# Decoder layer on one core: VectorE's share of the softmax exponentials, from 15 units of degree five in twelve passes to 19 units in eight instructions

## The chip, the cores and the metric

The kernel runs on one core of a Trainium2 chip. The metric is device time in microseconds (us) of one execution, as the median of several runs.

## What is computed

One decoder layer in float32: a small self-attention over distances, a cross-attention of 1024 query rows to 6404 context rows with 16 heads of width 8, and a quantized feed-forward part, each followed by a layer norm. Nearly all the time goes to the cross-attention:

```python
qh = split_heads(q @ Wq + bq)
kh = split_heads(k @ Wk + bk)
vh = split_heads(v @ Wv + bv)
logits = einsum('bhsd,bhtd->bhst', qh, kh) / sqrt(8)
attn = softmax(logits, axis=-1)
out = einsum('bhst,bhtd->bhsd', attn, vh)
```

These are 16 x 1024 x 6404, some 105 million exponentials.

## The kernel before

**Work.** A phase is one group of four heads and one half (512) of the query rows: eight phases. The 6404 context rows are 51 tiles of 128, in 17 chunks of three tiles (NC = 17). A tile and a head make one unit of 128 x 512 logits, one PSUM bank. Three units make a block: four blocks per chunk (BPC), three in the last chunk, 67 per phase, 536 in all. A block uses banks 0 to 2 or 3 to 5 by turns; banks 6 and 7 hold the accumulators. The logits are made with the context rows on the partitions, so the exponentials go straight into the values matmul; the row sums come from a column of ones beside the values.

**Engines.** TensorE goes through the blocks in order (`chunk`, L1320): it waits for the probabilities of two blocks before (probs_ready, L1340), writes a block's scores S (`scores`, twelve matmuls, L1284) and then does a part of the values V of the chunk before (`values`, L1314: eight matmuls of 512 for a tile, seen as 16 in the profile; the middle tile is done in two halves of 256 columns). ScalarE takes the exponential of each block in one instruction (`exponentials`, L706 to L712) of 1536 columns, or of 1024 where VectorE does the last unit. VectorE does that unit in the block s = 2 of 15 chunks of a phase (chunk 0 and chunks 2 to 15): `take` (L952) rounds the logit to an integer (e_t) and subtracts it (e_f), both out of PSUM; `power` (L970) evaluates a polynomial in the rest by Horner's rule (e_u) and multiplies it with the power of two (e_pow), which GpSimd makes from e_t (`powers`, L585). Every pass is cut into two halves of 256 columns, so that one half works while the result of the other becomes visible: twelve instructions. GpSimd also copies a chunk's values into v_op (`stage`, L577). The sync engine loads the keys (`load_k`, L279).

**Order and waits.** Before the first block of a chunk TensorE waits until VectorE has read the scores of the unit two blocks before (L1338, e_step), and before the values of the third tile until that unit's probabilities are written (L1365, e_probs). Chunks 2 to 13 run in a hardware loop of four chunks (KS) on TensorE, and of two on ScalarE; there the waits compare with registers. VectorE and GpSimd are written out. Between phases VectorE reads the accumulators (`add_acc`, L943; it needs the last values of the phase), and TensorE waits for that before the first values of the new phase (L1361).

```python
for s in range(LAST_BPC if c == NC - 1 else BPC):
    if s == 0 and c:
        wait(e_step, at(E_STEPS * (e_count(ph, c - 1) - 1) + E_TAKEN, E_STEPS))
    wait(probs_ready, at(f + s + 1, BPC))
    scores(m % KS, q, ph, c == NC - 1, s)
```

## Time and profile before

| | |
|---|---|
| median of 3 runs | 834.43 us (834.39 to 834.64) |
| profiled execution | 833.03 us |
| its span, first to last instruction | 831.3 us |
| mean granted TensorE clock | 0.967 |
| ScalarE busy | 736.0 us (89%) |
| TensorE busy | 707.7 us (85%) |
| VectorE busy | 689.5 us (83%) |
| GpSimd busy | 174.9 us (21%) |

The profile names the engines PE (TensorE matmuls), PEld (its weight loads), DVE (VectorE), ACT (ScalarE), POOL (GpSimd) and SP (sync). "L710" is line 710 of the kernel. A length in a timeline runs from the start of the first instruction of a row to the end of the last, xN is their count, and the brackets at its end tell how long the engine stood idle before it, and what ended that. Lengths of neighbours overlap: on ScalarE and VectorE the next instruction starts before the last one's results are all written.

### The profile page before, as it was taken

Reading aid. Unit: us, or ns where it says so; the run is one execution under the profiler, and the core shown is the slowest. Engines: PE = TensorE matmul, PEld = TensorE weight load, DVE = VectorE, ACT = ScalarE, POOL = GpSimd, SP = SyncE. Lnnn points to the kernel's source line nnn. Section 1 sums busy time; section 2 is a strip of 40 time slices with the busy share of each in tenths; the row PEclk is TensorE's granted clock in tenths of the full one; section 3 lists DMA queues with packets and bytes.
Section 4 is the critical chain, followed back from the end, with each engine's and each line's share of the span. In section 5 each row is a group of like instructions: output and inputs, shape, how many; then the busy total and the mean of one; then the engine's idle time right before and its main releaser. Section 6 shows DMA issues by size and latency. Waiting matters only on the chain.

```text
span 831.3 us, 38425 instructions
## 1 busy us (share of the span) xinstructions
PE 707.7 (85%) x15210; PEld 319.9 (38%) x15212; DVE 689.5 (83%) x1952; ACT 736.0 (89%) x650; POOL 174.9 (21%) x304
## 2 busy tenths in 40 slices
PE   6996679899899998899998999888899998899841
PEld 3445434443444344334443444344433443344321
DVE  3518767996999699969996999699978997899766
ACT  2436879999999999999999999999999999999741
POOL 2501511221222122212221222122212221222100
PEclk9998989999999999999999999999999999999965
DMA  3303521111111111111111111111111111111000
GB/s 105 83 25 107 170 86 37 37 43 44 38 36 45 42 37 38 43 43 38 36 44 43 36 37 40 44 38 35 40 48 35 37 37 49 37 36 38 14 1 26
DMA packets 36611, 38.41 MB, mean 46 GB/s; under 512 B 8430, under 2 KB 35088, under 8 KB 36512
## 3 DMA queue, kind: packets, MB, share of 16 engines
q1 hardware_dynamic: 35644, 36.59, 14.8%
q8 instruction: 65, 1.06, 0.5%
q10 hardware_dynamic: 868, 0.48, 0.2%
q14 instruction: 34, 0.28, 0.1%
HBM read 30.15 MB, written 6.42 MB: 44 GB/s over the span
## 4 chain that ended last, share of the span: by engine, by line
ACT 40%; issue 24%; PE 16%; SPq 10%; DVE 5%; DMA 3%; POOL 1%; ACTq 1%; POOLq 0%; DVEq 0%
ACT probs L710 39%; SPq L291 8%; PE ps L1314 6%; PE ps L1284 3%; PE ps L1213 2%; PE ps L1199 2%; DMA k_op<-k_parts_dram 2%; SPq L505 1%; DMA k_parts_dram<-k_parts 1%; PE ps L1162 1%; DVE stats L776 1%; PE ps L1449 1%; ACTq L723 1%; POOL k_parts L541 0%; DMA q_parts_dram<-q_parts 0%
## 5 line engine op out<-in xcount | busy, mean ns | idle before, releaser
L710 ACT ACTIVATE probs<-ps 128x1536 f32<-128x1536 f32 (+1 forms) x536 | 671.7, 1379 | 11.9 <-PE ps L1284 11.4
L1314 PE MATMUL ps<-probs,v_op 64*9 64x512 f32 (+1 forms) x8384 | 523.5, 494 | 13.8 <-DMA k_op<-k_parts_dram 9.1
L1284 PE MATMUL ps<-q_op,k_op 59*32 59x512 bf16 x6432 | 337.4, 382 | 60.7 <-ACT probs L710 56.4
L979 DVE SCALAR_TENSOR_TENSOR e_u<-e_u,e_f 128x256 f32<-128x256 f32 x720 | 259.2, 425 | 0.0
L1284 PEld LDWEIGHTS ps<-q_op,k_op 59*32 59x32 bf16 x6432 | 107.9, 90 | 331.5 <-issue 245.7
L1314 PEld LDWEIGHTS ps<-probs,v_op 64*9 64x9 f32 x8384 | 169.3, 86 | 90.2 <-issue 27.7
L588 POOL TENSOR_SCALAR e_pow<-e_t 128x512 int32<-128x512 int16 x120 | 74.4, 620 | 353.9 <-DVE e_t L960 353.9
L960 DVE TENSOR_SCALAR e_t<-ps 128x256 f32<-128x256 f32 x240 | 90.5, 418 | 60.5 <-PE ps L1284 51.3
L581 POOL COPY v_op<-v_all 128x108 f32<-128x108 f32 x136 | 68.3, 502 | 181.3 <-PE ps L1314 180.6
L979 DVE SCALAR_TENSOR_TENSOR e_u<-e_f 128x256 f32<-128x256 f32 x240 | 90.1, 416 | 0.2
L986 DVE SCALAR_TENSOR_TENSOR probs<-e_u,e_pow 128x256 f32<-128x256 f32 x240 | 89.6, 411 | 0.0
L966 DVE SCALAR_TENSOR_TENSOR e_f<-ps,e_t 128x256 f32<-128x256 f32 x240 | 89.2, 413 | 0.0
L541 POOL TENSOR_TENSOR k_parts<-probs,k_parts 128x384 bf16<-128x384 f32 x17 | 17.6, 1038 | 66.2 <-ACT k_parts L640 66.2
L667 ACT ACTIVATE probs<-ps,neg_n 128x1024 f32<-128x1024 f32 x8 | 8.9, 1113 | 16.8 <-PE ps L1213 16.8
L1162 PE MATMUL ps<-ctx_t,wk_turned 128*128 128x384 f32 x34 | 16.6, 571 | 6.3 <-ACT ctx_t L619 3.3
L1009 DVE STREAM_TRANSPOSE att_rows<-acc_t 128x512 f32<-128x512 f32 x7 | 5.0, 711 | 15.6 <-DMA o_t<-att_rows 15.6
L627 ACT ACTIVATE kf<-ps,bias_cols 128x384 f32<-128x384 f32 x17 | 9.8, 578 | 8.9 <-PE ps L1162 8.9
L1165 PEld LDWEIGHTS ps<-wv_sb,ctx_t 128*128 128x128 f32 x102 | 15.5, 208 | 5.2 <-issue 1.2
L1213 PE MATMUL ps<-y_rhs,y_lhs 64*128 64x512 f32 x32 | 15.6, 611 | 0.7 <-DVE v_all L811 0.7
L811 DVE TENSOR_TENSOR v_all<-ps,bv_bc 128x384 f32<-128x384 f32 (+1 forms) x17 | 9.4, 555 | 7.8 <-PE ps L1165 7.8
L640 ACT ACTIVATE k_parts<-probs 128x384 bf16<-128x384 f32 x17 | 8.8, 519 | 8.0 <-DVE probs L826 8.0
L1199 PE MATMUL ps<-probs,x_nat 128*128 128x512 f32 x32 | 15.6, 615 | 0.0
(177 smaller groups left out, 257.7 us busy)
## 6 DMA issues: line engine op xcount, KB each, us to landing
k_op<-k_parts_dram SPq DMA_DIRECT2D x544, 36.0 KB
k_parts_dram<-k_parts SPq DMA_DIRECT2D x17, 288.0 KB, 2.5
k_op<-k_parts_dram SPq DMA_DIRECT2D x272, 12.0 KB
ctx_nat<-in_ctx_dram SPq DMA_DIRECT2D x16, 192.0 KB, 2.6
q_op<-q_parts_dram SPq DMA_DIRECT2D x32, 48.0 KB
q_parts_dram<-q_parts SPq DMA_DIRECT2D x2, 384.0 KB, 3.4
x_nat<-in_x_dram SPq DMA_DIRECT2D x1, 512.0 KB, 3.9
o_t<-att_rows SPq DMA_DIRECT2D x28, 16.0 KB
```

Of the source, the lines that this page charges most:

```text
L291: sp.dma_start(k_op[W2 * r + a:W2 * r + a + DH * copies, slot, :, :].rearrange("p i t -> p (i t)"), bass.AP(src.tensor, starts[part][r], [ ...
L581: pool.tensor_copy(v_op[:, slot].rearrange("p j (h d) -> p j h d", h=G), v_all[:, bass.ds(tile, CT), head:head + G, :]).then_inc(v_staged, 1)
L588: pool.tensor_scalar(e_pow[:], e_low(e_t[:]), float(2 ** 23), float(EXP2_LEAD), ALU.mult, ALU.add).then_inc(e_pow_ready, 1)
L710: act.activation(probs[:, b % NP].rearrange("p u t -> p (u t)")[:, 0:columns], ps[:, bank:bank + BU, :].rearrange("p u t -> p (u t)")[:, 0 ...
L960: dve.tensor_scalar(e_t[:, cols], score, E_MIN, ROUND, ALU.max, ALU.add).then_inc(e_step, 1)
L966: dve.scalar_tensor_tensor(out=e_f[:, cols], in0=score, scalar=E_MIN, in1=e_low(e_t[:, cols]), op0=ALU.max, op1=ALU.subtract).then_inc(e_s ...
L979: dve.scalar_tensor_tensor(out=e_u[:, cols], in0=u[:, cols], scalar=a, in1=e_f[:, cols], op0=ALU.add, op1=ALU.mult).then_inc(e_step, 1)
L986: dve.scalar_tensor_tensor(out=probs[:, block % NP, BU - 1, 512 - EW + cols.start:512 - EW + cols.stop], in0=e_u[:, cols], scalar=EXP2[0], ...
L1199: last = pe.matmul(ps[:, 4 + b, :], x_nat[:, j, :], attn_e[:, j, HQ * b:HQ * b + HQ], start=(j == 0), stop=(j == TQ - 1), skip_group_check ...
L1213: last = pe.matmul(ps[:, 2 * (j % 2) + b, :], y_lhs[:, P * j:P * j + P], y_rhs[:, HQ * b:HQ * b + HQ], start=True, stop=True)
L1284: return pe.matmul(ps[a:a + P // G, bank, :], k_op[W2 * r:W2 * r + KR, kslot, i, P * j + a:P * j + a + P // G], q_op[W2 * r:W2 * r + KR, q ...
L1314: last = pe.matmul(ps[32 * k:32 * k + DH + 1, ACC[h], a:b], v_op[W2 * h:W2 * h + W2, slot, j, (DH + 1) * k:(DH + 1) * (k + 1)], probs[W2 * ...
```

## The change

VectorE makes 19 units per phase instead of 15, at places listed in E_AT (chunk, block): (0, 0), then in each turn of four chunks the blocks (0, 2), (1, 1), (2, 0), (2, 3), (3, 2), and at the end (14, 2), (15, 1), (16, 0). In these blocks ScalarE has 1024 columns. The polynomial is evaluated in another form: u = (f + a) f in two halves, f' = (u + c) f in two halves, f' scaled as (f' + d) times the power of two in one pass of 512 (`scale`), and the product (u + b) times that in one pass of 512 (`finish`). Rounding and remainder (e_t, e_f) are one pass of 512 each, so a unit has eight instructions. The scale of a unit is issued behind e_t of the next one, and the finish behind its e_f; e_f, e_u and e_pow have two buffers, in memory shared with qf and qr. ScalarE's loop has four chunks. TensorE waits for e_taken two blocks behind each unit, and makes the values of a tile between six and eight blocks after the tile's scores. After the last block the values of two more tiles are left, and the last ones wait for the last unit.

```diff
--- before.py
+++ after.py
@@ -74,16 +74,21 @@
 QSCALE = SCALE * LOG2E
 EW = 512
 EH = EW // 2
-E_BLOCK = BPC - 2
-E_UNITS = NC - 2
-EXP2_LEAD = 0x3aae0400
-EXP2 = [753.2197875976562, 522.0919799804688, 180.93934631347656,
-        41.8090705871582, 7.287810325622559]
+E_LOOP = 4
+E_TURN = ((0, 2), (1, 1), (2, 0), (2, 3), (3, 2))
+E_FIRST = 2
+E_AT = ([(0, 0)] + [(c + k, t) for c in range(E_FIRST, NC - 3, E_LOOP) for k, t in E_TURN] +
+        [(NC - 3, 2), (NC - 2, 1), (NC - 1, 0)])
+E_UNITS = len(E_AT)
+EXP2_OFF = 2
+EXP2_LEAD = 0x3a8bec00 - EXP2_OFF * 2 ** 23
+EXP2 = [9.525652885437012, 28.199888229370117, 45.54460906982422, 132.23011779785156]
 E_MIN = -116.0
-E_STEPS = 12
-E_TAKEN = 4
+E_STEPS = 5
+E_AHEAD = 1
...
+        q_work = sb("q_work", [P, 4, HQ])
...
+        qf, qr = q_work[:, 0:2, :], q_work[:, 2:4, :]
+        e_f = [e_f0[:], q_work[:, 0, :]]
+        e_u = [e_u0[:], q_work[:, 1, :]]
+        e_pow = [e_pow0[:], q_work[:, 2, :].bitcast(I32)]
...
+            def powers(ph, c, t):
+
+                n = e_count(ph, c, t)
+                pow2 = e_pow[n % 2]
+                if n > 2:
+
+                    pool.wait_ge(e_probs, E_AHEAD + n - 2)
+                pool.wait_ge(e_rounded, n)
+                pool.tensor_scalar(pow2, e_low(e_t[:]), float(2 ** 23), float(EXP2_LEAD),
                                    ALU.mult, ALU.add).then_inc(e_pow_ready, 1)
 
             for ph in range(PHASES):
                 for c in range(NC):
                     m = ph * NC + c
-                    stage(m % 2, m, c * CT, ph % NG * G)
-                    if c != 1 and c < NC - 1:
-                        powers(ph, c)
+                    for t in range(BPC):
+                        if t == 2:
+                            stage(m % 2, m, c * CT, ph % NG * G)
+                        if (c, t) in E_AT:
...
+                f = ph * BPP + c * BPC
+                for t in range(LAST_BPC if c == NC - 1 else BPC):
+                    count = f + t + 1 + AHEAD
+                    exponentials(f + t, count if i is None else i * (E_LOOP * BPC) + count,
+                                 BU * 512 - EW if (c, t) in E_AT else BU * 512)
 
             for ph in range(PHASES):
-                f = ph * BPP
-                for s in range(BPC):
...
-                    exponentials(f + s, f + (s + 1 + AHEAD))
-                with act.Fori(0, E_UNITS // 2) as r:
-                    for s in range(2 * BPC, 4 * BPC):
-                        exponentials(f + s, r * (2 * BPC) + (f + s + 1 + AHEAD), shared(s % BPC))
-                for s in range((NC - 1) * BPC, BPP):
-                    exponentials(f + s, f + (s + 1 + AHEAD))
+                for c in range(E_FIRST):
+                    chunk(ph, c)
+                with act.Fori(0, (NC - 3 - E_FIRST) // E_LOOP) as i:
+                    for c in range(E_FIRST, E_FIRST + E_LOOP):
+                        chunk(ph, c, i)
...
+            def make_probs(ph, at, before):
+
+                def score(block):
+                    return ps[:, BU * (block % 2) + BU - 1, :]
+
+                n = e_count(ph, *at)
+                block = ph * BPP + at[0] * BPC + at[1]
+                f, u = e_f[n % 2], e_u[n % 2]
+                if n > 1:
+
+                    dve.wait_ge(e_pow_ready, n - 1)
                 dve.wait_ge(scores_done, block + 1 + AHEAD)
+                dve.tensor_scalar(e_t[:], score(block), E_MIN, ROUND + EXP2_OFF, ALU.max, ALU.add
+                                  ).then_inc(e_rounded, 1)
+                if before:
+                    scale(*before)
+                dve.wait_ge(e_rounded, n)
+                dve.scalar_tensor_tensor(out=f, in0=score(block), scalar=E_MIN, in1=e_low(e_t[:]),
+                                         op0=ALU.max, op1=ALU.subtract).then_inc(e_taken, 1)
+                if before:
+                    finish(*before)
+                for i, cols in enumerate(halves):
+                    dve.wait_ge(e_taken, n)
+                    dve.scalar_tensor_tensor(out=u[:, cols], in0=f[:, cols], scalar=EXP2[0],
+                                             in1=f[:, cols], op0=ALU.add, op1=ALU.mult
...
+                for i, cols in enumerate(halves):
+                    dve.wait_ge(e_step, E_STEPS * (n - 1) + i + 1)
+                    dve.scalar_tensor_tensor(out=f[:, cols], in0=u[:, cols], scalar=EXP2[2],
+                                             in1=f[:, cols], op0=ALU.add, op1=ALU.mult
+                                             ).then_inc(e_step, 1)
+
+            def scale(ph, at):
+
+                n = e_count(ph, *at)
+                f = e_f[n % 2]
+                dve.wait_ge(e_pow_ready, n)
+                dve.wait_ge(e_step, E_STEPS * (n - 1) + 4)
+                dve.scalar_tensor_tensor(out=f, in0=f, scalar=EXP2[3], in1=e_pow[n % 2].bitcast(F32),
+                                         op0=ALU.add, op1=ALU.mult).then_inc(e_step, 1)
+
+            def finish(ph, at):
+
+                n = e_count(ph, *at)
+                block = ph * BPP + at[0] * BPC + at[1]
+                dve.wait_ge(e_step, E_STEPS * n)
+                dve.scalar_tensor_tensor(out=probs[:, block % NP, BU - 1, :], in0=e_u[n % 2],
+                                         scalar=EXP2[1], in1=e_f[n % 2], op0=ALU.add, op1=ALU.mult
+                                         ).then_inc(e_probs, 1)
...
+                for n, at in enumerate(E_AT):
+                    make_probs(ph, at, (ph, E_AT[n - 1]) if n > 1 else
+                               (ph - 1, E_AT[-1]) if ph and n == 0 else None)
+                    if n == 0:
+                        scale(ph, at)
+                        finish(ph, at)
+                        if ph:
+                            add_acc(ph - 1)
+                            turn_acc()
+                            if ph > 1:
+
+                                dve.wait_ge(o_written, 16 * G * (ph - 1))
+                            dve.transpose(att_rows[:], acc_t[:].rearrange("p n d -> p (n d)")
+                                          ).then_inc(att_ready, 1)
+            scale(PHASES - 1, E_AT[-1])
+            finish(PHASES - 1, E_AT[-1])
...
-            def chunk(ph, c, i=None, reach=0):
+            def chunk(ph, c, i=None):
...
                 def at(count, step):
-                    return count if i is None else pe.to_reg(i * (reach * step) + count)
+                    return count if i is None else pe.to_reg(i * step + count)
...
+                def wait_unit(signal, ahead, ph_u, c_u, t):
+
+                    turn = 0 if i is None else 1
+                    if (c_u + turn * E_LOOP, t) in E_AT:
+                        n = e_count(ph_u, c_u + turn * E_LOOP, t) - turn * len(E_TURN)
+                        wait(signal, at(ahead + n, len(E_TURN)))
+
+                def made(back, j, a=0, b=HQ, count=1, first=False):
+
+                    ph_v, c_v = (ph, c - back) if c >= back else (ph - 1, c - back + NC)
+                    if ph_v < 0:
+                        return
+                    if j == 0:
+
+                        wait(v_staged, at(m - back + 1, KS))
+                    if a == 0:
+                        for t in range(BPC):
+                            if (t * BU + BU - 1) // G == j:
+                                wait_unit(e_probs, E_AHEAD, ph_v, c_v, t)
+                    values((m - back) % 2, ph_v * BPP + c_v * BPC, j, c_v == NC - 1, count, first, a, b)
+
                 for s in range(LAST_BPC if c == NC - 1 else BPC):
-                    if s == 0 and c:
-
-                        wait(e_step, at(E_STEPS * (e_count(ph, c - 1) - 1) + E_TAKEN,
-                                        E_STEPS))
-                    wait(probs_ready, at(f + s + 1, BPC))
+                    if c or s >= 2:
+                        wait_unit(e_taken, 0, ph, *((c, s - 2) if s >= 2 else (c - 1, s + 2)))
+                    elif ph:
+                        wait_unit(e_taken, 0, ph - 1, NC - 1, s + 1)
+                    wait(probs_ready, at(f + s + 1, KS * BPC))
                     scores(m % KS, q, ph, c == NC - 1, s)
...
-                        wait(v_staged, at(m, 1))
+                        wait(k_loaded[(m + 1) % KS], at(K_LOAD * ((m + 1) // KS + 1), K_LOAD))
                     if c == 0:
-                        if s < CT:
-                            values(slot, f - LAST_BPC, s, True, count=2 if s == 1 else 1)
-                    elif c == NC - 1:
-                        if s == 2:
-                            pe.wait_ge(e_probs, 2 * e_count(ph, c - 1))
-                        values(slot, f - BPC, s, False, count=2 if s == 1 else 1)
+                        if s < 2:
+                            made(2, s + 1, count=2 - s)
+                        else:
+                            made(1, s - 2, count=s - 1)
+                    elif c == 1 and s < 2:
+                        if s == 0:
+                            made(2, 2)
                     elif s == 0:
+                        made(2, 1, a=HQ // 2)
+                    elif s == 1:
+                        made(2, 2)
+                    elif s == 2:
                         if c == 1 and ph:
 
                             pe.wait_ge(acc_step, ACC_STEPS * (ph - 1) + 2)
-                        values(slot, f - BPC, 0, False, first=c == 1)
-                    elif s == 3:
-
-                        wait(e_probs, at(2 * e_count(ph, c - 1), 2))
-                        values(slot, f - BPC, 2, False)
+                        made(1, 0, first=c == 1)
                     else:
-                        values(slot, f - BPC, 1, False, a=(s - 1) * (HQ // 2), b=s * (HQ // 2))
+                        made(1, 1, b=HQ // 2)
...
+            last_m = PHASES * NC - 1
+            pe.wait_ge(e_probs, E_AHEAD + E_UNITS * PHASES - 1)
+            for j in range(1, CT):
+                values((last_m - 1) % 2, BLOCKS - LAST_BPC - BPC, j, False, count=3 - j)
             pe.wait_ge(o_written, 16 * G * NG)
             pe.wait_ge(probs_ready, BLOCKS + 1)
             project_out(0)
             pe.wait_ge(v_staged, PHASES * NC)
+            pe.wait_ge(e_probs, E_AHEAD + E_UNITS * PHASES)
             for j in range(CT):
                 pe.wait_ge(probs_ready, BLOCKS + min(j + 1, 2))
-                values((PHASES * NC - 1) % 2, BLOCKS - LAST_BPC, j, True, count=2 if j == 1 else 1)
+                values(last_m % 2, BLOCKS - LAST_BPC, j, True, count=2 if j == 1 else 1)
```

The old `take` and `power` (L952 to L989) go, and so does the old order of the phase on VectorE (L1000 to L1012).

## Rows read from the trace of the kernel before

**Rows 1.** The page of the profile, part 1: busy time of each engine.
```profile
PE 707.7 (85%) x15210; PEld 319.9 (38%) x15212; DVE 689.5 (83%) x1952; ACT 736.0 (89%) x650; POOL 174.9 (21%) x304
```

**Rows 2.** Windows, phase 2: length, then busy PE, PEld, DVE, ACT, POOL; clock.
```profile
275.25:359.26 84.01, 76.00 (x1862) 32.76 (x1852) 75.81 (x216) 83.81 (x69) 17.25 (x32) 1.00 0.14 40
```

**Rows 3.** Windows, the steady loop of phase 3 (twelve chunks), columns as before.
```profile
372.26:431.53 59.27, 53.66 (x1356) 24.68 (x1344) 58.10 (x168) 59.27 (x49) 13.65 (x24) 1.00 0.13 38
```

**Rows 4.** Timeline of ACT, one chunk: start us, length us, instruction.
```profile
381.22 1.47 ACT L710 ACTIVATE probs<-ps 128x1536 f32<-128x1536 f32 x1
382.55 1.05 ACT L710 ACTIVATE probs<-ps 128x1024 f32<-128x1024 f32 x1
383.50 1.45 ACT L710 ACTIVATE probs<-ps 128x1536 f32<-128x1536 f32 x1
384.84 1.45 ACT L710 ACTIVATE probs<-ps 128x1536 f32<-128x1536 f32 x1
386.17 1.47 ACT L710 ACTIVATE probs<-ps 128x1536 f32<-128x1536 f32 x1
387.50 1.05 ACT L710 ACTIVATE probs<-ps 128x1024 f32<-128x1024 f32 x1
```

**Rows 5.** Timeline of PE, the same chunk: L1284 scores, L1314 values.
```profile
381.49 0.61 PE L1284 MATMUL ps<-q_op,k_op 59*32 59x512 bf16 x12 [0.18 <-ACT probs L710]
...
382.84 0.61 PE L1284 MATMUL ps<-q_op,k_op 59*32 59x512 bf16 x12 [0.30 <-ACT probs L710]
...
384.04 0.61 PE L1284 MATMUL ps<-q_op,k_op 59*32 59x512 bf16 x12
384.35 1.16 PE L1314 MATMUL ps<-probs,v_op 64*9 64x512 f32 x16
385.21 0.62 PE L1284 MATMUL ps<-q_op,k_op 59*32 59x512 bf16 x12
385.56 0.70 PE L1314 MATMUL ps<-probs,v_op 64*9 64x256 f32 x16
```

**Rows 6.** Timeline of DVE, the same chunk.
```profile
382.15 0.76 DVE L960 TENSOR_SCALAR e_t<-ps 128x256 f32<-128x256 f32 x2
382.82 0.74 DVE L966 SCALAR_TENSOR_TENSOR e_f<-ps,e_t 128x256 f32<-128x256 f32 x2
```

**Rows 7.** Groups by line and shape, whole execution: busy us, mean ns; idle before.
```profile
L710 ACT ACTIVATE probs<-ps 128x1536 f32<-128x1536 f32 x416 | 575.4, 1471 | 11.9 <-PE ps L1284 11.4
...
L979 DVE SCALAR_TENSOR_TENSOR e_u<-e_u,e_f 128x256 f32<-128x256 f32 x720 | 259.2, 425 | 0.0
...
L588 POOL TENSOR_SCALAR e_pow<-e_t 128x512 int32<-128x512 int16 x120 | 74.4, 620 | 353.9 <-DVE e_t L960 353.9
L960 DVE TENSOR_SCALAR e_t<-ps 128x256 f32<-128x256 f32 x240 | 90.5, 418 | 60.5 <-PE ps L1284 51.3
```

**Rows 8.** Line L979 in the steady loop: shortest, median and longest duration in ns.
```profile
L979 DVE SCALAR_TENSOR_TENSOR e_u<-e_u,e_f x72: 409/414/495, 374.3 to 430.4; 128x256 f32<-128x256 f32 x72
```

**Rows 9.** Timeline of DVE at the start of phase 4: two dependent passes of 512.
```profile
446.79 0.68 DVE L946 COPY acc_sb<-ps 128x512 f32<-128x512 f32 x1
447.50 0.69 DVE L947 TENSOR_TENSOR acc_sb<-acc_sb,ps 128x512 f32<-128x512 f32 x1
```

**Rows 10.** Timeline of all engines where TensorE was held by e_f.
```profile
397.66 0.74 DVE L966 SCALAR_TENSOR_TENSOR e_f<-ps,e_t 128x256 f32<-128x256 f32 x2
...
398.79 0.64 PE L1284 MATMUL ps<-q_op,k_op 59*32 59x512 bf16 x12
...
400.04 0.62 PE L1284 MATMUL ps<-q_op,k_op 59*32 59x512 bf16 x12
```

**Rows 11.** List of waits, whole execution: us in total, times, longest us.
```profile
PEld ps L1284 <- DVE e_f L966: 15.7, 32, 1.0
```

**Rows 12.** Timeline of ACT and of PE at the end of the last phase.
```profile
778.55 5.57 ACT L710 ACTIVATE probs<-ps 128x1536 f32<-128x1536 f32 x4
...
784.20 2.79 PE L1314 MATMUL ps<-probs,v_op 64*9 64x512 f32 x40
```

More of the change, by code:

```diff
@@ L170, in decoder_layer @@
         e_t = sb("e_t", [P, EW])
-        e_f = sb("e_f", [P, EW])
-        e_u = sb("e_u", [P, EW])
-        e_pow = sb("e_pow", [P, EW], I32)
+        e_f0 = sb("e_f", [P, EW])
+        e_u0 = sb("e_u", [P, EW])
+        e_pow0 = sb("e_pow", [P, EW], I32)
         acc_sb = sb("acc_sb", [P, HQ])
@@ L236, in decoder_layer @@
         acc_step, e_step, e_probs = sem("acc_step"), sem("e_step"), sem("e_probs")
+        e_rounded, e_taken = sem("e_rounded"), sem("e_taken")
         e_pow_ready = sem("e_pow_ready")
@@ L266, in row_bc, with e_count @@
             return bass.AP(v.tensor, v.offset, [[0, P], [1, ap.shape[0]]])
-        def e_count(ph, c):
-            return ph * E_UNITS + max(c - 1, 0) + 1
+        def e_count(ph, c, t):
+            return ph * E_UNITS + sum(at <= (c, t) for at in E_AT)
         def e_low(ap):
@@ L869, in _ @@
             chain.step(dve.memset(gmax[:], 0.0))
+            dve.sem_inc(e_probs, E_AHEAD)
             dve.wait_ge(attn_e_ready, TQ)
@@ L1318, in values, with chunk @@
                 last.then_inc(values_done, count)
-            def chunk(ph, c, i=None, reach=0):
+            def chunk(ph, c, i=None):
                 m = ph * NC + c
@@ L1376, in _ @@
                     for c in range(2, 2 + KS):
-                        chunk(ph, c, i, KS)
+                        chunk(ph, c, i)
                 for c in range(NC - 3, NC):
```

60 lines of the change are left out of this document (4 added, 56 removed).

## The prediction

> **What bounds the kernel now.** First the busy table and the windows of the phases. ScalarE leads with 736.0 of 831.3 us [rows 1], and most of the time is eight phases of some 84 us in which it is busy throughout: 83.81 of 84.01 us [rows 2]. In the steady loop (chunks 2 to 13) it never stops, 59.27 of 59.27 us, with VectorE right behind (58.10) and TensorE at 53.66 [rows 3]. A microsecond taken off ScalarE there is a microsecond gained, if neither of the others takes its place. Both are near, so the next thing to read is the handover between the engines, in one chunk of four blocks.
>
> There ScalarE starts the short block b (1024 columns) at 382.55, b+1 at 383.50, b+2 at 384.84, b+3 at 386.17 and the next short one at 387.50 [rows 4]: 0.94 us for a short block, then 1.35, 1.33 and 1.33 for full ones, 4.95 in all. The difference, 0.39, is what one more unit on VectorE saves ScalarE.
>
> Scores S go into two sets of three PSUM banks by turns, so S(b+2) may not start before everybody has read block b. TensorE starts S(b) at 381.49, S(b+1) at 382.84, S(b+2) at 384.04 and S(b+3) at 385.21; the first two had waited for ScalarE [rows 5], which ended block b at 382.55 + 1.05 = 383.60 and b+1 at 384.95 [rows 4]. A block of scores whose banks come free last starts 0.15 after that end: for S(b+1) that end is b-1's, at some 382.69 (381.22 + 1.47). From the start of S to the first instruction that reads it 0.66 us pass: VectorE's e_t of block b starts at 382.15 [rows 6], ScalarE's b+1 at 383.50.
>
> VectorE's unit is now twelve passes of 256. From e_t at 382.15 to the end of e_f at 382.82 + 0.74 = 383.56 it takes 1.41 us; with that the scores are taken. Independent passes of 256 start 0.335 apart (0.67 for two) [rows 6], though each lasts about 0.42 [rows 7]. While GpSimd copies v_op, one pass lasts 0.495 instead of 0.414 [rows 8]: 0.08 more in each chunk.
>
> Call D the start of e_t of unit block b. ScalarE, undisturbed, starts b+2 at 384.84 = D + 2.69. For that S(b+2) must start by D + 2.03. Now it starts at D + 1.89. **The slack is 0.14 us**, and on this point all else turns.
>
> **The change part by part.** (1) ScalarE: four more short blocks per phase, 32 in all, at 0.39 each: 12.5 us less work.
>
> (2) VectorE's unit becomes two passes of 512 on PSUM (e_t, e_f), two of 512 in SBUF (scale, finish) and four of 256. No row has independent 512-wide passes. From below: 256 columns start 0.335 apart, and from 256 to 512 the duration goes from 0.42 to 0.69 [rows 7, 9], 0.27 more, so 0.60. From above: 0.71, the distance of COPY and the TENSOR_TENSOR that needs its result [rows 9]. The change puts another pass between most that depend on each other, which is nearest to the independent rows: 0.60. The unit is 4 x 0.60 + 4 x 0.335 = 3.75, with the copy's share 3.80. Per 16 blocks that is 5 x 3.80 = 19.0, about the 4 x 4.77 of now (12 x 0.335, the gaps to e_t and the copy's share; the page's busy share says the same, 58.10 in twelve chunks).
>
> (3) The order inside a unit is e_t, scale of the unit before, e_f, finish of the unit before. So the scores are taken at D + 0.60 + 0.60 + 0.69 = D + 1.89, not D + 1.41. In its loop TensorE waits first on e_taken, then on probs_ready, both against registers. What such a pair costs when e_f is last stands once in the steady stretch: e_f ends at 397.66 + 0.74 = 398.40 and S starts at 398.79, 0.39 later [rows 10]; 32 waits of this kind are in the list of the whole execution [rows 11]. So S(b+2) starts at D + 2.28 and ScalarE's b+2 at D + 2.94, **0.25 us late**, on an engine without slack. From below: with only the 0.15 that ScalarE's end costs, S(b+2) starts at D + 2.04, on the edge of the slack. The 0.39 is of the same wait, so I take it.
>
> (4) Behind that late S, TensorE is in order: values, then S(b+3), which in four cases of five belongs to the next unit. With a full set of values (16 matmuls of 512) S to S is 1.25 after a late start [rows 10]. With a half set (16 of 256) the next S could start 0.30 before the values end, as it does behind a full one (384.35 + 1.16 against 385.21): 385.56 + 0.70 - 0.30 - 385.21 = 0.75 [rows 5].
>
> (5) One turn of the loop is 16 blocks with units at blocks 2, 5, 8, 11 and 14: distances 3, 3, 3, 3 and 4. ScalarE alone would need 0.94 + 1.35 + 1.33 = 3.62 for a distance of 3. The next e_t comes at the later of VectorE's 3.80 and TensorE's 2.28 + V + 0.66:
> - first and second: a half set follows, 3.69, so VectorE decides: 3.80 each.
> - third and fourth: a full set follows: 4.19 each.
> - the long one: ScalarE starts b+2 at 2.94, ends it 1.45 later [rows 4]; S(b+4) follows at 4.54, e_t at 5.20. VectorE would be free at 3.80 and waits, so what was lost is not won back.
>
> The sum is 21.18 us for 16 blocks, now 4 x 4.95 = 19.79: +1.39, in 24 turns **+33.4 us**.
>
> (6) The other 19 blocks of a phase take 84.0 - 3 x 19.79 = 24.6 now [rows 2]. Then: 3.80 and 3.80, a third distance into the next phase between 3.87 (wait 0.15, full set 1.17) and 4.19, taken as 4.0 because the waits are against constants there, and from unit (0,0) to unit (2,2) ten blocks, one short: 10 x 1.335 - 0.39 = 13.0. Again 24.6: nothing. The accumulators are read two blocks later, and chunk 1 starts on them two blocks later. GpSimd's powers are used a unit after they are made. Both cost nothing under that cover; without it the powers would put their 0.62 plus a handover into each unit.
>
> (7) Tail: the last exp ends at 778.55 + 5.57 = 784.12 and the 40 last value matmuls start at 784.20 [rows 12]. Afterwards the last unit lies on block 533, and without a following unit it ends at D + 3.75 + two dependent passes of 512 (1.45) and a handover, some 5.3, while ScalarE ends at D + 4.2: +1.1.
>
> 833.03 + 33.4 + 1.1 = 867.5 for the profiled execution, which lies 1.4 below the median of the runs: **869 us**.
>
> [...] e_t reads PSUM and lasts 0.418 per 256 columns, e_u works in SBUF alone and lasts 0.425 [rows 7]: PSUM has no price of its own here. [...]
>
> **Rivals.**
> - *Faster: the take is early enough.* If S(b+2) starts by D + 2.03 and a unit takes no more than 3.62, ScalarE stays the bound throughout and only the 12.5 us count: 822. For it: VectorE's work per turn, 19.0, fits under ScalarE's 11 x 1.335 + 5 x 0.94 = 19.39. Against it: the average is not what is asked; three blocks leave 3.62 and a unit takes 3.75 even with no wait. 0.11.
> - *Half of it: TensorE passes it on faster.* With 0.15 for the wait and 1.17 for a full set the distances are 3.80, 3.80, 3.87, 3.87 and 4.96, 20.30 per turn, +12.2, with the tail 848. I count 847 to 855 here: 0.15.
> - *More: the 512-wide passes don't overlap.* At 0.67 apart (two of 256) the unit is 4.10, the take at 2.03: 4.10, 4.10, 4.33, 4.33 and 5.34, 22.2 per turn, +58, 893. Beyond 882: 0.05.
> - *The values wait.* A finish ends 2.5 after the next e_t, 6.7 after its own, and its values are due six blocks, 8 us, after: 1.3 to spare. 0.01.
>
> The forecast, 855 to 882, keeps 0.68. The range takes it and the smaller case in, 847 to 882. Within 0.2% (about what a measurement of this kernel can tell from no change) lies only an accident between the first two cases: 0.02. Faster 0.11, slower 0.87.
>
> **What would show it.** Right: ScalarE's idle time before L710, 11.9 us now [rows 7], rises to some 45, ended by TensorE's scores; TensorE waits on e_f in nearly every unit of the loop, some 120 times; e_t starts 3.8, 3.8, 4.2, 4.2 and 5.2 apart; passes of 512 start 0.60 apart; a phase lasts 88 us. Wrong: ScalarE without idle time in the loop and phases of 82.4 (the first rival), or e_f ending before D + 1.7.

## The result: 855.17 us against 834.53, and the profile after

| | before | after |
|---|---|---|
| median | 834.53 us (834.39 to 834.76, 4 runs) | 855.17 us (854.08 to 856.41, 4 runs) |
| ratio, 95% interval | | 1.0244 (1.0226 to 1.0262) |
| span of the profiled execution | 831.3 us | 853.0 us |
| ScalarE, TensorE, VectorE, GpSimd busy | 736.0, 707.7, 689.5, 174.9 | 738.4, 718.7, 694.5, 275.6 |

The kernel is 2.4% slower; that it would be slower was forecast. The size is 20.6 us where 34.5 were forecast, and 855.2 lies at the very edge of the likeliest case (855 to 882), inside the range of 847 to 882.

ScalarE has 32 short passes more and is still counted busy for 2.4 us longer. The passes themselves became shorter, 1335 ns in the mean of 536 against 1379. But a pass of 1.46 us that is followed at once shares 0.12 us with the next one (they start 1.33 to 1.35 apart in [rows 4]), and one that is followed by a wait is counted in full.

The windows of the kernel after, as in [rows 2] and [rows 3]: phases 0, 2 and 3, and one turn of the loop (16 blocks) in phase 2; length first, then busy PE, PEld, DVE, ACT and POOL.

```profile
101.07:191.21 90.14, 76.38 (x1790) 30.23 (x1784) 73.58 (x152) 84.27 (x67) 31.83 (x37) 0.92 0.17 51
312.78:333.78 21.00, 18.18 (x456) 7.43 (x448) 19.05 (x40) 20.01 (x17) 7.81 (x9) 1.00 0.13 36
...
278.65:365.90 87.25, 77.42 (x1865) 30.79 (x1852) 76.24 (x159) 84.16 (x68) 30.39 (x36) 1.00 0.14 39
365.90:453.91 88.01, 77.87 (x1865) 30.74 (x1852) 76.24 (x159) 84.26 (x68) 30.39 (x36) 1.00 0.14 39
```

In [rows 3] ScalarE had no idle time in the loop; now it stands still for 0.99 of 21.00 us. Each other engine has spare time (VectorE 1.95, TensorE 2.82), and none is the bound by its share. A turn was 4 x 4.947 = 19.79 and is 21.00; a phase was 84.01 and is 87.25.

The timeline of VectorE in that turn, as in [rows 6]: the second unit whole, the starts of the others.

```profile
316.53 0.68 DVE L984 TENSOR_SCALAR e_t<-ps 128x512 f32<-128x512 f32 x1
317.13 0.68 DVE L1010 SCALAR_TENSOR_TENSOR q_work<-q_work 128x512 f32<-128x512 f32 x1
317.73 0.68 DVE L989 SCALAR_TENSOR_TENSOR e_f<-ps,e_t 128x512 f32<-128x512 f32 x1
318.33 0.68 DVE L1018 SCALAR_TENSOR_TENSOR probs<-q_work 128x512 f32<-128x512 f32 x1
318.93 0.75 DVE L995 SCALAR_TENSOR_TENSOR e_u<-e_f 128x256 f32<-128x256 f32 x2
319.60 0.75 DVE L1000 SCALAR_TENSOR_TENSOR e_f<-e_u,e_f 128x256 f32<-128x256 f32 x2
320.27 0.68 DVE L984 TENSOR_SCALAR e_t<-ps 128x512 f32<-128x512 f32 x1
...
321.47 0.68 DVE L989 SCALAR_TENSOR_TENSOR q_work<-ps,e_t 128x512 f32<-128x512 f32 x1
...
324.48 0.69 DVE L984 TENSOR_SCALAR e_t<-ps 128x512 f32<-128x512 f32 x1 [0.31 <-PE ps L1318]
...
328.56 0.69 DVE L984 TENSOR_SCALAR e_t<-ps 128x512 f32<-128x512 f32 x1 [0.25 <-PE ps L1318]
```

Passes of 512 start 0.60 apart and last 0.68. From e_t to the end of e_f it is 318.41 - 316.53 = 1.88 us. The starts of e_t are 3.74, 4.21 and 4.08 apart here, 3.75 ahead of the first and 5.22 behind the last (it ends at 333.78): forecast were 3.80, 3.80, 4.19, 4.19 and 5.20. In the first two distances (3.75 and 3.74) VectorE never waits; ahead of the e_t at 324.48 and the one at 328.56 it waits for TensorE.

TensorE and ScalarE around the same unit, as in [rows 5] and [rows 4]:

```profile
318.75 0.61 PE L1318 MATMUL ps<-q_op,k_op 59*32 59x512 bf16 x12
...
319.53 0.61 PE L1318 MATMUL ps<-q_op,k_op 59*32 59x512 bf16 x12
...
322.50 0.61 PE L1318 MATMUL ps<-q_op,k_op 59*32 59x512 bf16 x12
322.87 1.10 PE L1348 MATMUL ps<-probs,v_op 64*9 64x512 f32 x16
323.73 0.64 PE L1318 MATMUL ps<-q_op,k_op 59*32 59x512 bf16 x12
```

```profile
317.93 1.46 ACT L727 ACTIVATE probs<-ps 128x1536 f32<-128x1536 f32 x1
319.41 1.45 ACT L727 ACTIVATE probs<-ps 128x1536 f32<-128x1536 f32 x1
```

Call the time from the end of the take to the start of the scores that waited for it the handover. The scores two blocks on start at 318.75 and 322.50, 0.34 and 0.35 after the end of e_f (318.41, 322.15). ScalarE starts that block at 319.41 = D + 2.88, 1.48 behind the one before instead of 1.33 to 1.35. Behind the second late start a full set of values follows, and the next scores come 1.23 later.

From the list of waits of the whole execution, against the one row in [rows 11]:

```profile
PE ps L1318 <- DVE q_work L989: 26.7, 37, 2.8
ACT probs L727 <- PE ps L1318: 24.8, 68, 1.7
PE ps L1318 <- DVE e_f L989: 24.0, 36, 1.1
...
PEld ps L1318 <- DVE q_work L989: 20.9, 20, 3.4
PEld ps L1318 <- DVE e_f L989: 18.6, 20, 1.0
...
PE ps L1348 <- DMA k_op<-k_parts_dram: 0.4, 1, 0.4
```

The four rows with L989 (e_f in either buffer) add up to 113 entries, where some 120 waits were forecast, but that is not a count of units: some waits stand there twice, for the matmul and for its weight load (0.30 and 0.80 for the scores at 356.36), and some not at all, because TensorE's values end just as the scores start (at 322.48 for those at 322.50). Counted from the starts, the first 14 of the 15 units of a loop have a handover of 0.34 or 0.35 us almost without exception (102 of 112, and all but one of the others at most 0.40): the take holds TensorE in nearly every unit.

The code outside the loop, where the waits compare with constants, hands over faster. Unit (14, 2) of phase 2, the first one behind the loop, is an example:

```profile
355.62 0.68 DVE L989 SCALAR_TENSOR_TENSOR q_work<-ps,e_t 128x512 f32<-128x512 f32 x1
356.36 0.61 PE L1318 MATMUL ps<-q_op,k_op 59*32 59x512 bf16 x12 [0.30 <-DVE q_work L989]
```

e_f ends at 356.30 and the scores start 0.06 later. All 40 units whose scores two blocks on lie outside the loop (five per phase) have 0.05 or 0.06.

### The profile page after: what moved, and what is told of

It is laid out like the page before. It is cut to its first block, busy times and chain, and to the rows that moved or that the text cites. A ratio compares the mean times of both kernels' runs of the same rounds, so it can differ in the third digit from the quotient of the medians.

```text
span 853.0 us, 38088 instructions
## 1 busy us (share of the span) xinstructions
PE 718.7 (84%) x15212; PEld 302.7 (35%) x15212; DVE 694.5 (81%) x1488; ACT 738.4 (87%) x650; POOL 275.6 (32%) x336
## 4 chain that ended last, share of the span: by engine, by line
PE 49%; DVE 21%; issue 12%; ACT 12%; SPq 2%; POOL 2%; DMA 1%; DVEq 0%; ACTq 0%; POOLq 0%
PE ps L1348 22%; PE ps L1318 19%; ACT probs L727 10%; DVE e_f L1010 4%; DVE q_work L1010 4%; DVE e_f L989 3%; DVE q_work L989 3%; PE ps L1247 2%; PE ps L1233 2%; SPq L301 2%; DVE probs L1018 1%; DVE e_t L984 1%; DVE e_u L995 1%; DVE q_work L995 1%; POOL v_op L591 1%
## 5 line engine op out<-in xcount | busy, mean ns | idle before, releaser
L727 ACT ACTIVATE probs<-ps 128x1536 f32<-128x1536 f32 (+1 forms) x536 | 673.9, 1335 | 29.3 <-PE ps L1318 24.8
L984 DVE TENSOR_SCALAR e_t<-ps 128x512 f32<-128x512 f32 x152 | 104.5, 687 | 87.4 <-PE ps L1318 86.4
L603 POOL TENSOR_SCALAR q_work<-e_t 128x512 int32<-128x512 int16 x76 | 68.2, 897 | 118.6 <-DVE e_t L984 90.2
L995 DVE SCALAR_TENSOR_TENSOR e_u<-e_f 128x256 f32<-128x256 f32 x152 | 58.6, 426 | 0.1
L995 DVE SCALAR_TENSOR_TENSOR q_work<-q_work 128x256 f32<-128x256 f32 x152 | 58.6, 426 | 0.2
L1000 DVE SCALAR_TENSOR_TENSOR q_work<-q_work 128x256 f32<-128x256 f32 x152 | 57.1, 415 | 0.0
L1000 DVE SCALAR_TENSOR_TENSOR e_f<-e_u,e_f 128x256 f32<-128x256 f32 x152 | 57.0, 415 | 0.0
L1010 DVE SCALAR_TENSOR_TENSOR e_f<-e_f,e_pow 128x512 f32<-128x512 f32 x76 | 51.7, 680 | 0.5
L1010 DVE SCALAR_TENSOR_TENSOR q_work<-q_work 128x512 f32<-128x512 f32 x76 | 51.7, 680 | 0.4
L989 DVE SCALAR_TENSOR_TENSOR q_work<-ps,e_t 128x512 f32<-128x512 f32 x76 | 51.9, 682 | 0.2
L989 DVE SCALAR_TENSOR_TENSOR e_f<-ps,e_t 128x512 f32<-128x512 f32 x76 | 51.8, 682 | 0.1
L1018 DVE SCALAR_TENSOR_TENSOR probs<-e_u,e_f 128x512 f32<-128x512 f32 x76 | 51.7, 680 | 0.2
L1018 DVE SCALAR_TENSOR_TENSOR probs<-q_work 128x512 f32<-128x512 f32 x76 | 51.7, 680 | 0.1
```

The source lines that it names most:

```text
L603: pool.tensor_scalar(pow2, e_low(e_t[:]), float(2 ** 23), float(EXP2_LEAD), ALU.mult, ALU.add).then_inc(e_pow_ready, 1)
L727: act.activation(probs[:, b % NP].rearrange("p u t -> p (u t)")[:, 0:columns], ps[:, bank:bank + BU, :].rearrange("p u t -> p (u t)")[:, 0 ...
L984: dve.tensor_scalar(e_t[:], score(block), E_MIN, ROUND + EXP2_OFF, ALU.max, ALU.add).then_inc(e_rounded, 1)
L989: dve.scalar_tensor_tensor(out=f, in0=score(block), scalar=E_MIN, in1=e_low(e_t[:]), op0=ALU.max, op1=ALU.subtract).then_inc(e_taken, 1)
L995: dve.scalar_tensor_tensor(out=u[:, cols], in0=f[:, cols], scalar=EXP2[0], in1=f[:, cols], op0=ALU.add, op1=ALU.mult).then_inc(e_step, 1)
L1000: dve.scalar_tensor_tensor(out=f[:, cols], in0=u[:, cols], scalar=EXP2[2], in1=f[:, cols], op0=ALU.add, op1=ALU.mult).then_inc(e_step, 1)
```

## The experiments

Ten more kernels were run, in three groups; each ratio is to the kernel before on the same chip. Six of the medians (swap to old_take5) rest on two runs each, so small differences are read from the distances. D is the start of a unit's e_t. The distances named are those of successive e_t in an undisturbed turn of the loop, each taken from that run's trace.

| run | median us | before, same chip | ratio | one turn of the loop, us |
|---|---|---|---|---|
| swap | 844.1 | 833.8 | 1.0123 (1.0094 to 1.0153) | 3.75, 3.74, 4.01, 3.88, 5.03 = 20.41 |
| early | 861.5 | 833.8 | 1.0332 (1.0237 to 1.0426) | 3.88, 3.95, 3.94, 3.94, 5.03 = 20.74 |
| four | 851.8 | 833.8 | 1.0216 (1.0175 to 1.0257) | 4 x 5.22 = 20.9 |
| four_early | 847.5 | 833.8 | 1.0164 (1.0134 to 1.0193) | 4 x 5.04 = 20.2 |
| old_take6 | 874.9 | 833.4 | 1.0498 (1.0451 to 1.0544) | 4 x 5.35 = 21.4 |
| old_take5 | 845.3 | 833.4 | 1.0143 (0.998 to 1.0305) | 4 x 5.01 = 20.0 |
| four_early2 | 835.7 | 833.4 | 1.0045 (1.0004 to 1.0086) | 4 x 4.95 = 19.8 |
| wide512 | 836.1 | 833.4 | 1.0024 (1.0008 to 1.0039) | 3.74, 3.81, 3.81, 3.73, 4.97 = 20.06 |
| four_wide_swap | 836.4 | 834.8 | 1.0027 (1.0002 to 1.0051) | 4 x 4.98 = 19.9 |
| old_swap | 835.2 | 834.8 | 1.0001 (0.9979 to 1.0024) | 4 x 4.95 = 19.8 |

### The handover: swap

```diff
 for s in range(LAST_BPC if c == NC - 1 else BPC):
+    wait(probs_ready, at(f + s + 1, KS * BPC))
     if c or s >= 2:
         wait_unit(e_taken, 0, ph, *((c, s - 2) if s >= 2 else (c - 1, s + 2)))
     elif ph:
         wait_unit(e_taken, 0, ph - 1, NC - 1, s + 1)
-    wait(probs_ready, at(f + s + 1, KS * BPC))
     scores(m % KS, q, ph, c == NC - 1, s)
```

> TensorE's two waits ahead of the scores two blocks behind a unit change places: probs_ready first, e_taken last. Nothing else. Theory (the late take costs, and 0.39 us of it is the pair of waits): with e_taken last only some 0.15 us lie between the end of e_f and the scores, so the distances fall from 3.75, 3.74, 4.21, 4.08, 5.22 to 3.75, 3.74, 3.97, 3.84, 4.98, 20.3 us for 16 blocks instead of 21.0, and the time falls by 24 x 0.72 = 17 us to 838. Rival (VectorE's unit of 3.75 in a distance that leaves ScalarE 3.62 is all of the loss): no change, 855.

Exchanging the two waits takes 11 us off. The trace of swap, VectorE and TensorE:

```profile
318.15 0.68 DVE L989 SCALAR_TENSOR_TENSOR q_work<-ps,e_t 128x512 f32<-128x512 f32 x1
```

```profile
318.98 0.61 PE L1318 MATMUL ps<-q_op,k_op 59*32 59x512 bf16 x12
```

e_f ends at 318.83 and the scores start 0.15 later. The three distances that TensorE sets fell by 0.20, 0.20 and 0.19, and the two that VectorE sets did not move: just the split of the prediction. The rival in which only the unit's length counts is out.

The gain is smaller than the 17 us expected for two reasons. The handover in the loop had been 0.35 and not 0.39. And outside the loop the exchange makes it longer, as the same unit of phase 2 shows in swap:

```profile
351.39 0.68 DVE L989 SCALAR_TENSOR_TENSOR q_work<-ps,e_t 128x512 f32<-128x512 f32 x1
352.23 0.61 PE L1318 MATMUL ps<-q_op,k_op 59*32 59x512 bf16 x12 [0.39 <-DVE q_work L989]
```

That is 0.16 instead of 0.06, though the order of the waits is now the one that helps inside the loop. The distance at the way out of the loop became 4.94 from 4.85, and the third one at the end of a phase 4.05 from 3.96. Each of the two reasons is good for some 3 of the 6 us that are missing.

### The moment of the take, in the kernel before: old_take6 and old_take5

```diff
-E_TAKEN = 4
+E_TAKEN = 6
```

> The kernel before, with one number changed: TensorE waits for step 6 of a unit instead of step 4 (E_TAKEN 6 for 4), so it is told 0.67 us later that the scores are read, at D + 2.08. VectorE and ScalarE do exactly what they did. Theory: the scores two blocks on start at D + 2.08 + 0.39 = D + 2.47, ScalarE can bear D + 2.03, so 0.44 is lost per unit of the loop (12 a phase) and about 0.25 in the three others: 6 us a phase, 48 in all, 882. Rival (VectorE's unit length and load is what counts, not the moment of the take): 834.

```diff
-E_TAKEN = 4
+E_TAKEN = 5
```

> As the run before, with step 5: TensorE is told 0.335 us later, at D + 1.75, and the scores start at D + 2.14. Theory: only what lies beyond the slack of 0.14 over the start of now is lost, 0.11 per unit in the loop: 12 x 0.11 x 8 = 10.6 us, 845. If there were no slack, 0.335 less the 0.08 by which TensorE is later anyway: 0.25 per unit, 859. Rival (moment of the take does not count): 834.

These two hold everything of the change away except the moment at which TensorE is told. A chunk of 4.947 became 5.01 and 5.35, so the loss per chunk is 0.06 and 0.40 where 0.11 and 0.44 were expected. The second step of 0.335 costs 0.34 in full, the first one 0.06, so 0.27 of it was slack. VectorE's and ScalarE's work is that of the kernel before, and yet old_take6 is 41 us slower, more than the whole change. The start of an undisturbed chunk of old_take5:

```profile
400.65 0.76 DVE L960 TENSOR_SCALAR e_t<-ps 128x256 f32<-128x256 f32 x2 [0.17 <-PE ps L1284]
402.75 0.61 PE L1284 MATMUL ps<-q_op,k_op 59*32 59x512 bf16 x12
```

The scores start at D + 2.10, 0.35 after a take at D + 1.75. So the handover of the two register waits is 0.34 to 0.35 in this kernel too, and not the 0.39 of [rows 10].

The change moves the take by 1.89 - 1.41 = 0.48, from which 0.21 would follow by this slope, and the long distance shows 5.22 - 4.95 = 0.27. The rest lies at the other end: where VectorE waits for the scores, its e_t starts 0.73 to 0.75 behind them in the change and 0.66 in the kernel before. The two timed runs of old_take5 lie apart (839.6 and 851.0), so its 845 as expected says little, and the distances carry the verdict. The rival in which the moment does not count (834) is out by old_take6.

### Fewer units, same take: four

```diff
-E_TURN = ((0, 2), (1, 1), (2, 0), (2, 3), (3, 2))
+E_TURN = ((0, 2), (1, 2), (2, 2), (3, 2))
```

> Four units in 16 blocks (block 2 of each chunk) instead of five, 16 per phase; the unit's code stays, with its late take. Every distance in the loop is four blocks. Theory: each take is 0.25 us late and each distance is what the long one is now, 5.22, so 20.9 us for 16 blocks against 21.0 with five units: about 853, though VectorE has over a microsecond to spare in each unit. Rival (VectorE's load or unit length is the bound): distances of 4.95, 19.8 us for 16 blocks, 855 - 24 x 1.2 = 826 to 834.

With a unit less in 16 blocks VectorE waits 1.4 us in each unit, and the chunk still takes 5.22, as expected. The rival in which VectorE's load is the bound (4.95) is out. VectorE's starts in this run:

```profile
399.42 0.69 DVE L984 TENSOR_SCALAR e_t<-ps 128x512 f32<-128x512 f32 x1 [1.40 <-PE ps L1318]
404.64 0.69 DVE L984 TENSOR_SCALAR e_t<-ps 128x512 f32<-128x512 f32 x1 [1.39 <-PE ps L1318]
```

So the fifth unit of a turn is worth nothing as the change makes it: 20.9 with four, 21.0 with five.

### The take moved forward: early, four_early, four_early2

In early the two passes that read PSUM come first; four_early is the same with four units.

```diff
                 dve.tensor_scalar(e_t[:], score(block), E_MIN, ROUND + EXP2_OFF, ALU.max, ALU.add
                                   ).then_inc(e_rounded, 1)
-                if before:
-                    scale(*before)
                 dve.wait_ge(e_rounded, n)
                 dve.scalar_tensor_tensor(out=f, in0=score(block), scalar=E_MIN, in1=e_low(e_t[:]),
                                          op0=ALU.max, op1=ALU.subtract).then_inc(e_taken, 1)
                 if before:
-                    finish(*before)
+                    scale(*before)
                 for i, cols in enumerate(halves):
                     dve.wait_ge(e_taken, n)
...
+                if before:
+                    finish(*before)
                 for i, cols in enumerate(halves):
                     dve.wait_ge(e_step, E_STEPS * (n - 1) + i + 1)
```

> VectorE's order becomes e_t, e_f, scale of the unit before, two halves of u, finish of the unit before, two halves of f'. The scores are taken at D + 1.41 instead of D + 1.89; e_f now waits for e_t directly, which makes the unit longer by 0.11, 3.87 us. Theory: TensorE is no longer late (scores at D + 1.80), every short distance is VectorE's 3.87 and the long one ScalarE's 4.95, 20.4 us for 16 blocks, 841 us in all. Rival (unit length alone): the longer unit makes it slower, 855 + 24 x 4 x 0.12 = 866.

> Four units in 16 blocks and the order that takes early (e_t, e_f, scale, u, finish, f'). Theory: the late take was all that cost in the run with four units, so distances of 4.95, 19.8 us for 16 blocks, and a time near the kernel before: 834 to 837. Rival (something else of the new code costs in every unit, the register waits or the shared memory of the buffers): the distances stay above 5.1.

Both missed: 861.5 us for 841, and 847.5 for 834 to 837. The turn of early, 20.74, is below the 21.00 of the change, not at the 21.48 of the rival, though the time lies near that rival's 866. In its short distances VectorE goes from pass to pass without a wait, and a unit takes 3.88 to 3.95 where 3.87 was expected. What the loop wins, 0.7 us per phase, is lost outside it: the first distance of a phase is 14.08 instead of 13.22, and the last three are 11.77 instead of 11.45 together. The spans are 856.4 and 853.0; by the two medians alone it is not shown that early is slower than the change, since their intervals against the kernel before touch.

And four_early has 5.04 where 4.95 was expected. The reason for this, and for the first distance of 14.08 in both, is in the waits. The values of TensorE wait for VectorE's finish (L1018): 90 entries in four_early (21.5 us at PE, 15.9 at PEld) and 76 in early (18.7 and 15.9), against 2 in the change. The wait is 1.4 to 1.7 us at the start of a phase, and 0.18 to 0.19 in the loop of four_early. The trace of four_early, VectorE and TensorE:

```profile
473.48 0.69 DVE L1018 SCALAR_TENSOR_TENSOR probs<-e_u,e_f 128x512 f32<-128x512 f32 x1
```

```profile
473.75 0.61 PE L1318 MATMUL ps<-q_op,k_op 59*32 59x512 bf16 x12
474.32 1.07 PE L1348 MATMUL ps<-probs,v_op 64*9 64x512 f32 x16
```

The finish moved behind both halves of u and ends at 474.17; the values start at 474.32, 0.57 behind their scores instead of 0.24. The expectation had priced the take and forgotten whoever waits for the pass that was pushed back. In four_early2 the finish goes between the halves of u, and in the first unit of a phase right behind the scale:

```diff
-                if before:
+                if before and False:
                     scale(*before)
...
-                if before:
+                if before and not False:
+                    scale(*before)
+                if before and (False or at == (0, 0)):
                     finish(*before)
                 for i, cols in enumerate(halves):
...
+                    if before and i == 0 and not (False or at == (0, 0)):
+                        finish(*before)
```

The scale now stands behind e_f and the finish between the halves of u.

> Four units in 16 blocks with the early take, but the finish of the unit before is issued between the two halves of u, not behind both and before f' (and right behind the scale in the first unit of a phase). In the run four_early the values at block b+7 started when the finish ended, 8.3 us after the unit's own e_t, and distances were 5.04. Theory: the finish ends 0.41 us earlier and the values no longer wait: 4.95 in the loop, the start of a phase back to 13.2, together 836 to 838. Rival (another cost of the new code in every unit): distances stay at 5.04.

The loop is back at 4.95 per chunk, the waits for the finish shrink to 14 entries (8.4 us), none of them in the loop, and the time is 835.7, from 851.8 with the late take. The start of a phase takes 13.46, not the 13.2 expected.

### What is left is the length of the unit: wide512

```diff
-halves = (slice(0, EH), slice(EH, EW))
+halves = (slice(0, EW),)
```

with E_STEPS 3 for 5, the order of four_early2 (e_t, e_f, scale, u, finish, f'), and the waits of swap.

> All 19 units, six passes of 512 (u and f' whole, not in halves), order e_t, e_f, scale, u, finish, f', and TensorE waits for e_taken last. A unit is 5 x 0.60 + 0.72 = 3.72, with GpSimd's share 3.80, the scores are taken at D + 1.41. Theory: the take no longer limits (scores at D + 1.56), but VectorE's 3.80 is over ScalarE's 3.62: distances 3.80 four times and 4.95, 20.15 us for 16 blocks against 21.0: 855 - 24 x 0.85 = 835, no faster than the kernel before with its 15 units. If the length of the unit did not matter once the take is early: 19.4 for 16 blocks, 822.

Nineteen units, 836.1 us, for 835 expected. The distances 3.74, 3.81, 3.81 and 3.73 are VectorE's own: in them it goes from pass to pass without a gap. In the long one, 4.97, it waits 1.15 us for TensorE.

```profile
464.82 0.68 DVE L984 TENSOR_SCALAR e_t<-ps 128x512 f32<-128x512 f32 x1
465.53 0.69 DVE L989 SCALAR_TENSOR_TENSOR e_f<-ps,e_t 128x512 f32<-128x512 f32 x1
466.14 0.68 DVE L1014 SCALAR_TENSOR_TENSOR q_work<-q_work 128x512 f32<-128x512 f32 x1
466.74 0.68 DVE L997 SCALAR_TENSOR_TENSOR e_u<-e_f 128x512 f32<-128x512 f32 x1
467.34 0.76 DVE L1022 SCALAR_TENSOR_TENSOR probs<-q_work 128x512 f32<-128x512 f32 x1
468.02 0.68 DVE L1004 SCALAR_TENSOR_TENSOR e_f<-e_u,e_f 128x512 f32<-128x512 f32 x1
468.63 0.68 DVE L984 TENSOR_SCALAR e_t<-ps 128x512 f32<-128x512 f32 x1
```

A pass that needs the one in front starts 0.71 behind it (e_t to e_f), the others 0.60 or 0.61, except behind the finish of 0.76, where it is 0.68. The turn is 0.27 above the 19.79 of the kernel before, so 19 units of this length win nothing over 15 even with an early take. The values wait for a finish here too, 23 times at PEld (10.4 us), though only once in a loop, so the 0.27 is not theirs; and seven times, at the start of a phase, for GpSimd's copy (4.9 us).

One distance of each phase shows what a shorter unit would give, in the change itself. The unit (2, 2) has no scale and no finish of another unit between its passes, so it has six instructions and its take is early. In phase 2:

```profile
291.84 0.69 DVE L984 TENSOR_SCALAR e_t<-ps 128x512 f32<-128x512 f32 x1 [3.58 <-PE ps L1318]
292.56 0.69 DVE L989 SCALAR_TENSOR_TENSOR e_f<-ps,e_t 128x512 f32<-128x512 f32 x1
295.44 0.69 DVE L984 TENSOR_SCALAR e_t<-ps 128x512 f32<-128x512 f32 x1 [0.73 <-PE ps L1318]
```

The scores are taken at D + 1.41, VectorE waits 0.73 for the next ones, and the distance is 3.60, that of ScalarE alone (3.62). In phases 1 to 7 it is 3.60 to 3.76. A whole loop of such units was not run.

### A version that beats both, and a control: four_wide_swap, old_swap

> The best of the parts together: four units in 16 blocks (16 a phase), six passes of 512 in the order that takes early, e_taken waited for last. The loop keeps its 4.95 per chunk, as in four_early2, because ScalarE is the bound there; only the three short distances at the end of a phase, 3.88, 3.95 and 3.95 in four_early2, become 3.74, 3.81 and 3.81, as in wide512: 0.42 a phase, 3.4 us less than four_early2, 832 to 833, within a microsecond of the kernel before with its 15 units. If the length of the unit counted in the loop too, the loop would fall below 4.95: not expected.

It does not beat the kernel before: 836.4 for the 832 to 833 expected, 1.0027 (1.0002 to 1.0051). The last distances are 3.74, 3.81 and 3.81 as expected, but the loop stands at 4.98 and not at 4.95, which takes back 2.9 of the 3.4 us. Where the 0.03 comes from is open.

```diff
+                    wait(probs_ready, at(f + s + 1, BPC))
                     if s == 0 and c:
 
                         wait(e_step, at(E_STEPS * (e_count(ph, c - 1) - 1) + E_TAKEN,
                                         E_STEPS))
-                    wait(probs_ready, at(f + s + 1, BPC))
```

> The kernel before with the same exchange as in the run swap: ahead of a chunk's first scores TensorE waits for probs_ready first and for e_step last. Theory: there the scores two blocks on start 0.14 before ScalarE would feel it even where e_f came last, so nothing is gained: within 0.3 us of the kernel before. If the order of the two waits were worth something by itself in each chunk (0.2 us of TensorE), the time would fall by up to 136 x 0.2 = 27 us, or by that part of it that ScalarE sees.

No difference, 1.0001 (0.9979 to 1.0024): in this kernel, where the take has slack, the exchange is worth nothing. No version that ran is faster than the kernel before, and only old_swap cannot be told from it.

## Why the prediction was right, and what it had too large

**The slack and the late take (step 3): right.** The take at D + 1.89 was measured at 1.88. The handover was 0.34 to 0.35 instead of 0.39, and ScalarE's next block came at D + 2.88 for D + 2.94. That it is the moment and not the load was shown by old_take5 and old_take6. The deadline, forecast as D + 2.03 for the start of the scores, comes out as the take of D + 1.41, its slack of 0.27 and the handover of 0.34 to 0.35: D + 2.02 to 2.03.

**The 512-wide pass (step 2): right.** It is 0.60 from start to start, and the rival with 0.67 is out. The passes that read PSUM last 687 and 682 ns (e_t, e_f), scale and finish in SBUF 680: the lengths are within 7 ns, and the next pass starts 0.60 behind either kind. So at 512 columns, as at 256 in [rows 7] (418 ns for e_t, 425 for e_u), PSUM has no price of its own here.

**The unit of the kernel before has fourteen instructions, not twelve.** [rows 3] have 168 in twelve chunks: two each for e_t and e_f, eight for the polynomial, two for the product. The 4.77 of step 2 is right, but it is 14 x 0.335 + 0.08 and not made from 12 x 0.335. Nothing else in the sum rests on the twelve.

**The distances of a turn (steps 4 and 5): right within 0.11**, 21.00 for 21.18. That VectorE decides the first two and TensorE the next three was confirmed by swap, which moved only those three. That the third and the long one lie within 0.02 of the forecast is in part luck: the scores start 0.04 to 0.06 earlier than forecast, and e_t starts 0.73 to 0.75 behind its scores and not 0.66.

**The rest of the phase and the tail (6, 7).** The end of a phase has 3.75, 3.74 and 3.96, for 3.80, 3.80 and 4.0. Its start takes 13.22 for 13.0. Undisturbed these 19 blocks take 24.68 us, before 24.63: nothing, as forecast. Outside the phases the time grew by 2.0, for 1.1.

**The signs.** Phases 1 to 6 last 87.25 to 88.01 us (88 forecast), but ScalarE's idle time before its passes (L727) rose from 11.9 only to 29.3 and not to 45.

**The step that was mis-sized is the sum +33.4 for the loops.** From the traces, 24 turns took 481.5 us before and 502.8 after: 21.3. Two things were wrong with 24 x (21.18 - 19.79).
- Behind the loop the code has constants in its waits, with the handover of 0.06: each third turn ends with 4.85 instead of 5.22. With that and the shorter distances of the loop three undisturbed turns take 21.00 + 21.00 + 20.63 = 62.6, for 63.5: 7.5 us over all phases.
- The kernel before did not spend 19.79 in each turn. It waited for keys from memory, above all in phase 0. From its list of waits:

```profile
PE ps L1314 <- DMA k_op<-k_parts_dram: 9.1, 8, 4.0
...
PEld ps L1314 <- DMA k_op<-k_parts_dram: 4.9, 6, 1.4
```

After, 0.4 is left of them on PE. Phase 0 was 90.29 and is 90.14, no longer at all, while phase 2 grew by 3.24. Eight undisturbed loops would take 474.2 before and 500.8 after, so there were 7.3 us of disturbance before and are 2.0 after: 5.3 us less, and phase 0 alone accounts for that (5.8 before, 0.5 after). 33.4 - 7.5 - 5.3 = 20.6, and 21.3 was measured; the rest is that the loop before also ends with a shorter distance, 4.86, and takes 59.27 and not 3 x 19.79. The prediction took the size of a phase from an undisturbed one and multiplied it by eight, though the table of the phases was at hand.

Why phase 0 waits less is open. It is not simply that a slower loop hides the wait: the longest wait for keys, about 122 to 125 us into each run, is 4.0 us before and 0.4 in the change, but 3.2 in early and 2.7 in four_early, which are slower than the kernel before as well, and in four_early2, whose loop has the pace of the kernel before, no wait for keys in phase 0 is longer than 1.0. For the waits in the later phases (up to 1.6 us each) the slower pace does fit: the seven traces with a span of 837.8 us or more have none after phase 0, and the five with 834.1 or less all have some. The 19 blocks outside the loops took 1.6 us less in all than before, and the whole is 21.3 - 1.6 + 2.0 = 21.7, the difference of the two spans.

**The faster rival** failed where it was said to: it asks for S(b+2) by D + 2.03 and for a unit under 3.62. four_early2 meets the first and has 19.8 per turn with four units, wide512 has the take too but not the length, and neither is faster. The distance of 3.60 behind unit (2, 2) has both; that both would be enough for a whole turn is argued and not shown.

**The rival of waiting values**, priced at 1.3 us to spare, did not occur in the loops of the change. It came in early and four_early at the start of a phase, and in four_early in the loop too: there the finish ends 0.8 to 0.9 later, and a distance of four blocks adds another 1.3.

## What to carry to other kernels

Where two engines read the same buffer, the one that gives it back last can set the pace, and the moment of its last read counts, not its load (told of it 0.67 us later, with the same work, the kernel before took 874.9 us instead of 833.4; with a unit less in 16 blocks a chunk of the change still took 5.22): put the passes that read the shared buffer first, and fill dependence gaps with other work only up to the slack, which is read from the start of the refill and the start of its reader. The order of two waits in a queue can matter: in the kernel after, with waits that compare with registers, putting last the one that comes last saved 0.20 us, and with constants the same exchange cost 0.09, so it has to be measured where it stands. Before multiplying a loss per turn by the number of turns, compare the undisturbed turn with the sum of all turns (474.2 and 481.5 us here): what lies between them need not be there after the change.
